# Another merged order of two batches' steps and the shared steps on all engines of a two-layer decoder kernel

## The reference

```python
x = _layernorm(x + L0_attn(x))            # hawk block: rms norm, convolution over 4 tokens, gates,
                                          #   h[t] = alpha[t] h[t-1] + xs[t], gelu, out; then a gated MLP
x = _layernorm(x + L0_xattn(x, ctx))      # cross attention, 8 heads, masked context
x = _layernorm(x + L0_ffn(x))             # latent attention (16 heads of 8, rope, causal), then a
                                          #   mixture of 7 experts (best 2, sigmoid router) and a shared one
x = _layernorm(x + L1_attn(x))            # selective scan, 16 states: h = A_bar h + Bx, y = C h
x = _layernorm(x + L1_xattn(x, ctx))      # cross attention with FiLM, diagonal state space applied as a
                                          #   convolution (K from exp(dt A), by FFT), MLP, layernorm
x = _layernorm(x + L1_ffn(x))             # mixture of 8 experts of 176 (best 2, softmax) and 2 shared ones
```

## Time and profile before

| what | us |
|---|---|
| median of 3 runs | 486.77 |
| lowest and highest run | 484.85, 487.86 |
| span of the profiled execution | 484.9 |
| TensorE, VectorE, ScalarE, GpSimd busy | 413.4, 333.5, 293.4, 125.2 |
| table loads on ScalarE, 42 of 1.28 | 53.9 |

### The profile page before, as it was taken

One profiled execution on the slowest core, in us unless ns is written; L12 is line 12 of the kernel. 1 busy time (PEld: TensorE's weight loads), 2 busy tenths in 40 slices (PEclk: granted clock), 3 DMA queues, 4 the chain that ended last, 5 costly groups with the idle time before them and its releaser, 6 DMA issues.

```text
span 484.9 us, 5925 instructions
## 1 busy us (share of the span) xinstructions
PE 413.4 (85%) x2035; PEld 202.0 (42%) x2035; DVE 333.5 (69%) x616; ACT 293.4 (61%) x508; POOL 125.2 (26%) x129
## 2 busy tenths in 40 slices
PE   5968988888889999999977875557889899999995
PEld 2443533443345554434343221232666544544442
DVE  1386567789969953562799999899977543564454
ACT  4865697526245678889576896456347575652125
POOL 1100000000382029007966667745000200000000
PEclk9999999958789999999997996667989999999999
DMA  8950000564181000005008857979500000501401
GB/s 280 341 153 30 1 2 0 170 90 150 50 191 25 2 4 3 2 15 161 0 18 239 211 168 214 213 206 278 230 0 1 1 0 17 159 1 53 123 0 43
DMA packets 26109, 46.62 MB, mean 96 GB/s; under 512 B 7397, under 2 KB 12742, under 8 KB 24918
## 3 DMA queue, kind: packets, MB, share of 16 engines
q1 hardware_dynamic: 25972, 46.15, 33.6%
q10 hardware_dynamic: 108, 0.10, 0.1%
HBM read 41.13 MB, written 5.01 MB: 95 GB/s over the span
## 4 chain that ended last, share of the span: by engine, by line
PE 58%; DVE 19%; ACT 12%; issue 5%; POOL 3%; DMA 2%; SPq 1%; DVEq 0%; ACTq 0%
ACT AR L1207 7%; DVE AR L1553 7%; PE PS L924 7%; PE PS L956 6%; PE PS L929 5%; PE PS L852 4%; PE PS L838 4%; PE PS L821 3%; ACT L1203 3%; PE PS L688 3%; PE PS L1007 2%; DVE stats L1562 2%; DVE AR L1559 2%; POOL AR L2195 2%; DVE AR L1878 2%
## 5 line engine op out<-in xcount | busy, mean ns | idle before, releaser
L1207 ACT ACTIVATE AR<-PS 128x512 f32<-128x512 f32 (+3 forms) x187 | 98.9, 563 | 103.3 <-PE PS L924 49.5
L1553 DVE TENSOR_TENSOR AR<-PS,AR 128x512 f32<-128x512 f32 (+1 forms) x104 | 69.1, 675 | 49.6 <-PE PS L929 30.4
L2195 POOL TENSOR_TENSOR AR<-AR 128x512 f32<-128x512 f32 (+2 forms) x48 | 52.5, 1101 | 137.3 <-DVE AR L1553 106.7
L1207 ACT ACTIVATE AR<-AR 128x256 f32<-128x256 f32 (+3 forms) x110 | 46.7, 463 | 44.3 <-DVE AR L1553 28.0
L1203 ACT ACT_TABLE_LOAD x42 | 53.9, 1283 | 0.8
L1562 DVE TENSOR_REDUCE stats<-PS 128x1 f32<-128x512 f32 (+4 forms) x88 | 43.6, 521 | 10.3 <-PE PS L762 4.3
L1878 DVE TENSOR_TENSOR_SCAN AR<-PS,AR 128x512 f32<-128x512 f32 x32 | 38.8, 1212 | 1.3 <-ACT PS L1207 0.7
L821 PE MATMUL PS<-RR 97*128 97x512 bf16 (+3 forms) x128 | 34.1, 344 | 4.2 <-DVE stats L1562 3.3
L688 PE MATMUL PS<-AR,W_sq 128*128 128x256 f32 x88 | 27.3, 424 | 10.8 <-ACT AR L1207 6.3
L1553 DVE TENSOR_TENSOR AR<-AR 128x512 f32<-128x512 f32 (+2 forms) x48 | 32.3, 689 | 3.9 <-ACT AR L1207 2.6
L1207 ACT ACTIVATE AR<-PS,W_vec 128x256 f32<-128x256 f32 (+1 forms) x46 | 24.2, 545 | 12.6 <-PE PS L688 4.3
(11 more groups left out here) (241 smaller groups left out, 712.8 us busy)
## 6 DMA issues: line engine op xcount, KB each, us to landing
AR<-scan SPq DMA_DIRECT2D x64, 256.0 KB, 3.9
RR<-in_ffn SPq DMA_DIRECT2D x1, 2688.0 KB, 11.1
RR<-in_ones SPq DMA_DIRECT2D x2, 832.0 KB
RR<-in_ones SPq DMA_DIRECT2D x2, 784.0 KB
RA<-in_moe SPq DMA_DIRECT2D x1, 1539.5 KB, 6.2
AR<-weights SPq DMA_DIRECT2D x6, 256.0 KB, 4.8
W_mla<-in_mla SPq DMA_DIRECT2D x1, 1504.0 KB, 15.9
W_late<-in_late SPq DMA_DIRECT2D x1, 1076.0 KB, 11.5
```

What stands on the lines that cost most here:

```text
L1207: nc.scalar.activation(out_, in_, func, bias=bias, scale=scale).then_inc(*done("act", *step))
L1553: nc.vector.tensor_tensor(out_, a, b_, op).then_inc(*done("dve", *step))
L2195: nc.gpsimd.tensor_tensor(out_, a, b_, op).then_inc(*done("pool", *step))
```

## The change

Only two tables are replaced: TURNS, the merged order of the four engines, and TABLES, the positions of ACT's table loads, 40 instead of 42. No step, no operation and no wait is added, removed or changed, and no lane's own order. Against the order before, the step at a position differs at 345 of 541 positions on PE, 291 of 465 on ACT, 450 of 575 on DVE and 46 of 97 on POOL. SP's queue is the same.

Where the larger moves go:

- The preparation for the state space stands earlier: on DVE z5 to z9 and a1 to a3 in the hawk stage, a4 to a6 behind a:X1, w2.s, w2.m, w2.c and sz in a's context attention, hd.s and hd.m among a's maxima; on ACT th, sh, sy directly behind b:cv1, ahead of a's ln1 squares; on POOL dc1 to sz ahead of b's split.
- In the hawk stage a:gr1, a:gr2 on PE ahead of b:z0, and a:shr ahead of b:z2; on ACT a:h4.ra and a:h4.r ahead of b:h1.la; on DVE a:in1 ahead of w:v0, a:gh1 ahead of w:m1, a:xx ahead of w:VF0.
- On PE a:mx0.A to a:mx0.D stand ahead of b:xa.t0, and b's v ahead of a:mx4.E; a's and b's maxima and score units interleave in another way, with a's last score units further ahead of b's.
- w:q1.1 ahead of a:hu7; r2.1, q2.1, rQ0.1 behind a:dl; P1 behind a:hc15; a:s4a ahead of b:sc0; a:X4a behind b:sc4 instead of b:sc3.
- On POOL U11 and U21 behind a:by6, V1 behind a:by12, b:dx behind a:by15.
- In the cross attention w:kl, fl0 and fl1 earlier; in the second experts a's steps mostly ahead of b's.

The diff, cut to the first and last lines of each engine's list:

```diff
 TURNS = {
     "pe":
-        "a8 w1 a5 w2 a2 w1 a3 w1 a4 w2 a2 b2 a1 b2 a2 b1 a2 b1 a2 b2 a2 b2 a2 b2 a2 b2 a1 b5 a1 b2 a3 b7 a1 b2 "
...
+        "a7 w1 a6 w2 a3 w1 a1 w1 a5 w2 a2 b2 a3 b1 a1 b1 a1 b1 a2 b2 a2 b3 a1 b1 a2 b3 a2 b5 a1 b2 a3 b5 a1 b4 a4 "
...
     "dve":
-        "a1 w2 a1 w1 a6 w2 a1 w9 a3 w2 a3 w1 a1 w1 a1 w2 a3 b2 w4 b3 a1 b1 a1 b1 w1 b1 w1 a12 b1 a1 b1 a1 b3 a1 "
-        "b2 a1 b1 w1 a1 w1 a1 b4 a2 w1 a4 b1 a1 b1 w1 a1 w2 a2 b11 a1 b1 a2 w1 a3 b2 a3 w1 a1 b2 a4 b2 a7 w1 a3 "
-        "b1 a1 b3 a19 w1 a4 b4 w1 b5 w1 b8 a1 b8 a1 b4 w1 b1 w1 b3 a1 b1 a1 b9 a1 b4 w1 b1 a1 w1 a2 w1 b1 a2 w1 "
...
+        "a1 w2 a1 w2 a7 w5 a1 w7 a6 w1 a2 w3 a2 w1 b1 w3 b1 w4 a1 b1 w2 a1 b5 w2 a2 w3 a1 w1 a1 w1 a5 b1 a4 b1 w1 "
+        "a1 b1 w1 b4 a1 b1 a3 b4 a6 b1 a1 b1 a3 b7 a1 b3 a1 b2 a5 b2 a5 b1 a3 b3 a3 w1 a3 b1 w1 b3 a23 b1 a4 b12 "
...
     "act":
-        "a4 b1 a2 w1 a2 w1 a1 w1 b1 a3 w1 a1 w2 a13 b1 a2 b3 a1 b2 a3 b1 a4 b1 a1 b1 a1 b6 a1 b1 a1 b1 a1 b3 "
...
+        "a3 w1 a1 b1 a2 w1 a1 w1 a1 b1 a1 w1 a1 w1 a2 w1 a16 b4 a2 b2 w3 a6 b2 a1 b1 a1 b7 a2 b3 a1 b1 a15 b3 a1 "
...
     "pool":
-        "w13 b3 w1 b2 w1 b1 w37 a1 w1 a4 w1 a7 w1 a4 b1 a1 w1 b16 w1",
+        "w39 b6 w13 a8 w2 a6 w1 a3 b1 w1 b16 w1",
 }
...
 TABLES = (
-    "2:log 11:gelu 12:log 14:gelu 17:exp 26:log 40:gelu 47:log 51:gelu 52:exp 64:log 91:gelu 100:log "
-    "125:sin 133:log 230:sin 232:exp 239:sin 245:exp 247:sin 254:log 272:sin 280:exp 282:sin 283:exp "
...
+    "2:log 13:gelu 14:exp 15:gelu 22:log 40:gelu 45:sin 49:log 53:gelu 55:exp 67:log 94:gelu 102:log 230:sin "
+    "233:exp 241:sin 248:log 251:sin 255:log 272:sin 280:exp 282:sin 283:exp 285:sin 286:exp 289:sin 292:exp "
...
```

## The result

The new order is slower: median 489.28 us (487.68 to 493.41, 9 runs) against 485.92 us before in the same rounds (484.35 to 487.86, 9 runs), a ratio of 1.0085 with an interval of 1.0053 to 1.0118. The forecast was 481.6 us. The time lies inside the range of 476 to 490, on the other side of no change than the forecast; the upper part of that range was kept for another cause, TensorE's clock, so that it lies inside is luck.

What follows compares the result with a forecast made beforehand. No engine bounds the whole; TensorE fills 145 to 180 and 390 to 474 us, elsewhere engines wait for each other. Terms -2.6 +1.9 -2.1 -1.3 +1.4 -1.8 -0.7 = -5.2 from 484.9, plus 1.9: 481.6 us; range 476 to 490.

Steps and rivals of the forecast that it cites:

- Hawk, -2.6: Start to a's X1 (58.7 us): reordered steps on VectorE, ScalarE and TensorE bring X1 2.6 us earlier.
- a's context attention, +1.9: 58.7 to 79.5 us: preparation steps put into VectorE's queue cost 1.9 us, leaving a:xm 0.7 earlier.
- The bounds were 0 and 4.9: Cost in us of VectorE and POOL waiting for each other beside POOL's moved chain; nothing of it was taken.
- Latents and maxima, -2.1: 79.5 to 141.0 us: preparation work leaving VectorE moves a's last maximum from -0.7 to -2.8 us.
- b's maxima, -1.3: Start of TensorE's full stretch: dc1, dc2 out of POOL's split bring b's maxima from -2.8 to -4.1 us.
- First experts, +1.4 and -1.8: From 207 us: q1.1 ahead of a:hu7 costs 1.4; r2.1, q2.1 behind a:dl give 1.8 by the first scan.
- Scan and tail, -0.7: Scan to 390 us: P1 behind a's last scan and a shorter X4 wait give 0.7 together; nothing moves after.
- the rival that gives part back: "Given back", 20%: a:s4a holds b's first scan by 2.2 us and the last 0.7 fails; 484.5 us.
- POOL and VectorE shut each other out: Rival, 8%: in a's context attention the full 4.9 us of mutual waiting is paid; -0.3, 486.5 us.
- The slower case: Rival, 10%: thinner TensorE work from 110 to 145 us runs at the low clock; +8, 494 us.
- Under 0.80 there: Sign against the forecast: a TensorE clock under 0.80 between 105 and 140 us would make it wrong.
- The 1.9 added: Step from the profiled span (484.9 us) to the median of three runs (486.77), added to 479.7 for 481.6.

Runs made afterwards that it cites:

- e4: New order up to 143 us, the order before for all behind it; ratio to the kernel before 1.0010 (0.9986 to 1.0034).
- e5: New order up to 200 us, the order before for all behind it; ratio to the kernel before 1.0044 (1.0018 to 1.0070).
- e12: New order up to 262 us, the order before for all behind it; ratio to the kernel before 1.0111 (1.0072 to 1.0150).
- e7: Kernel before with only the new a/b interleaving up to b's X1, preparation not moved; ratio 0.9936 (0.9905 to 0.9968), median 484.26 us.
- e8: Kernel before with only the state-space preparation moved to its new places; ratio 1.0170 (1.0135 to 1.0204).
- e10: Kernel before with only z5 to a6 and th, sh, sy moved; GpSimd's chain, w2, sz, hd left; ratio 1.0075 (1.0037 to 1.0113).
- e3: New kernel with the state-space preparation put back where the kernel before has it; ratio to before 1.0103 (1.0049 to 1.0156).
- e2: New kernel with two groups of b's matmuls put back between a's transposes and xa.o on TensorE; ratio to before 1.0088 (1.0055 to 1.0121).
- e13: New kernel with b's normalization and router earlier, eP0, eQ0, P0, r1.1, q1.1 behind a's experts; ratio to before 1.0291 (1.0246 to 1.0336).
- e14: New kernel with b's normalization and router earlier, but eP0 and eQ0 kept ahead of a:sl4; ratio to before 1.0171 (1.0140 to 1.0202).
- e1: New kernel with w:q1.1 behind a:hu7 and b:xf again, r2.1 and q2.1 behind a:X3; ratio to before 1.0083 (1.0054 to 1.0113).

## Why the prediction was wrong, point by point

The sum was made in steps, so it can be laid beside the cuts (ratio less 1, of 486 us):

| up to | forecast, us | measured, us |
|---|---|---|
| a's maxima, 143 | -2.8 | +0.5 (e4) |
| the score units, 200 | -4.1 | +2.1 (e5) |
| a's X3 and the first scan, 262 | -4.5 | +5.4 (e12) |
| the end | -5.2 | +4.1 |

- **Hawk, -2.6: right, and kept where it stands alone.** -1.8 to -4.2 at X1 in the traces with the new interleaving, and alone 0.64% (3.1 us) at the end (e7); with the rest of the new order up to 143 nothing of it is left there (e4). The preparation's functions among ScalarE's ln1, counted at +0.4 less 0.6, cost more: X1 is +1.9 in e8 and +0.9 in e10, where they move without the interleaving.
- **a's context attention, +1.9: mis-sized by 1.1 to 1.6.** From X1 to xm the traces with the whole preparation moved lose 3.0 (new), 3.3 (e5, e12), 3.5 (e4) and 3.4 (e8, where nothing else is moved); where GpSimd's chain, w2 and sz stand as before it is 0.0 (e10), 1.4 (e7) and 1.9 (e3). The low clock at xa.o isn't it: e2, without it, loses 3.3 too. The step that failed here is the one that took nothing for POOL and VectorE. The bounds were 0 and 4.9. In e8 VectorE's rows are 0.75 longer in three places (0.91, 0.95 and 0.95 instead of 0.69, 0.69 and 0.68) and POOL's chain 2.65, together 3.4, and w:sz did wait, 1.61; in the new kernel VectorE's are 0.7 longer in four places and the chain 2.0, with no wait. The argument for 0, that POOL's steps are short, was the wrong one: a step of 0.45 took up to 1.01 beside an operation of 0.69.
- **Latents and maxima, -2.1: didn't come.** From xm to a's last maximum the traces with the preparation moved show -0.4 (new), +1.5 (e12), +2.4 (e5), +2.9 (e4) and +3.4 (e8), those without it +0.1 (e7) and +0.5 (e3); e13 and e14, with the order of the new kernel there, show -0.9 and -0.8. None has the -2.1. The step that failed is the one that counted 3.2 us of VectorE work taken out as time; VectorE was busy for 29.25 of 35 there and wasn't the pace, as the prediction itself had read from that row. That TensorE's waits or the loads of the stacks are the pace there was not tried.
- **b's maxima, -1.3: b's first came early, b's last late.** -2.1 and +4.1 in the new kernel (VectorE's wait before b's first is 1.34 us, where under 1 was forecast and 2.61 stood before). The prediction looked only at when the full stretch begins and held that an order can change nothing inside it. It decides whose matmuls are done in it, and the stretch behind lost 1.38 us of TensorE (e4 against e5). Nor did the early start give what was counted: TensorE is full from 144, but at a granted clock of 0.50 from 144 to 146, where e5 has 1.00, and b's maxima lose 6.2 in the new kernel and 4.8 in e5.
- **First experts, +1.4 and -1.8: the largest miss.** The step that failed: the working followed VectorE's queue alone, the w steps that change places (q1.1, r2.1, q2.1), and put nothing for TensorE's queue, in which b's score units, late by then, stand ahead of a's experts and b:rt ahead of a:ln3.v. Forecast was -2.7 at a's X3; it is +6.3 in the new kernel's trace and +7.1 in e12's. Shown by runs: the loss lies between 200 and 262 (e12 against e5). Read from the traces: TensorE's queue, 2.3 us less of TensorE to 246, and a granted clock of 0.69 behind it. Not shown: which inversion sets it. q1.1 (e1) and b's normalization (e13, e14) were tried and aren't it, or not by themselves. That stays open.
- **Scan and tail, -0.7: within what can be told.** 0.9989 (0.9964 to 1.0014) for the new order there alone. In the new kernel a:s4a ahead of b's scan waits 0.51 us for TensorE, not the 2.2 of the rival that gives part back; b's first scan behind it then waits 1.53 for ScalarE (0.56 for POOL before).
- **The rivals.** "POOL and VectorE shut each other out" had its mechanism right and 8% of the chance; its price (486.5) lacked the losses behind 143. The slower case named the clock between 105 and 140, where it is 0.75 against 0.78 before; the clock fell instead behind a's experts (0.69 from 246 to 262). "Under 0.80 there" was no sign of anything, since before was under it already, and the case's own sum gives 494.5, not 494. No rival had the losses of the score units and the first experts. The prediction held that about 1% can be told from no change; the loss of 0.85% is told by an interval of 0.33% on either side.
- **The profiled execution.** Every run's time is its span plus about 1.8 us, so the span of 484.9 belongs to a run of 486.7, near the median, and not to the fastest run, beside which the text set it. The 1.9 added was right all the same.

## What to carry to other kernels

A new merged order is priced by cutting it: the new order to a moment, the old one behind it, with the moment moved on; the same stretch tried alone in the old surroundings cost twice the whole change. Work taken off an engine that wasn't full counted for nothing here, so ask first whether that engine sets the pace; and GpSimd work put beside VectorE's two-operand operations in SBUF came nearer the upper bound (3.4 of 4.9) than nothing. Inside a stretch where one engine is full, ask whose work it does first: as I read these traces, a lane that falls behind there leaves the engine without filler in the next stretch. Follow a moved step through every queue on its way, not only the one that it left. And look at several traces of one order before reading a difference between two: here they scatter by 2 to 3 us.

## What the runs showed of the hardware that was not expected

The stretches in which TensorE is granted the low clock move from execution to execution of the same program, and the span goes with them: three runs of the new kernel at a mean granted clock of 0.937, 0.922 and 0.915 have spans of 485.9, 489.1 and 491.6 us. In the profiled execution of the new kernel TensorE waits for 1.88 us at 243.3, and from 245.7 to 255.9 it runs at the lower level of 1.2 GHz, though it is busy for 13.49 of the 16 us there. In e1's profiled execution that wait is 0.60 and the clock from 246 to 262 is 0.79 instead of 0.69, and it still came out at 491.1 with a mean clock of 0.915: low stretches stood elsewhere (0.89 from 175 to 190, where the new kernel has 1.00).
